# Earlier LayerNorm statistics, a lower load threshold, and a split first output group

## The chip, the cores and the metric

The kernel runs on all 8 cores of one Trainium2 chip. Each core works on its own 2,048 tokens of 4,096 features and no core talks to another, but the cores share the memory outside. The metric is device time in microseconds of the slowest core; smaller is better.

## The reference

```python
x = x + attn(layernorm(x))     # causal convolution over the last axis (4096) with an S4 kernel K, plus D * u
x = x + ffn(layernorm(x))
# ffn, with 64 experts of rank 16, top 16 of them by score:
scores = xf @ Wr.T
top_vals, top_idx = jax.lax.top_k(scores, TOPK)
gates = jax.nn.softmax(top_vals, axis=-1)
G = zeros(N, K).at[arange(N)[:, None], top_idx].set(gates)
h = einsum('nd,krd->nkr', xf, A)
out = einsum('nkr,kdr->nd', h * G[:, :, None], B) * 2.0
```

The convolution kernel K comes from 64 complex state values by a Cauchy sum. The kernel on the chip works out K by matrix powers instead (the setup below).

## The kernel before

The core's tokens are cut into four groups of 512 (`s` = 0 to 3), held transposed: features lie on the partitions as 32 blocks of 128, tokens along the row. Instructions are written out per engine by a small class `Plan`: each engine runs its own list strictly in the order of emission, with waits on counting semaphores put in by hand. `P.dma` with its default makes each transfer wait for the one before it on the same semaphore.

**Setup.** Small tables are loaded; then SP loads group 0 of the input, `U`, in four quarters of 8 blocks each (L381, semaphore `uld`, one after the other). Then some 200 small steps build the convolution matrices. Each is issued by `so(engine, fn)`, which waits for the step before it (semaphore `seq`), whatever its engine: a serial chain through VectorE and TensorE. The first 43 steps are VectorE's and one ScalarE's alone; step 44 is the first TensorE one, the matmul at L444. Steps 44 to 47 are matmuls, 48 and 49 the copies L448 and L449, 50 the matmul L452. Later ones that matter here: 60 is L467 and 61 L468, 62 is L469; 71 is L483, 72 is L484, 73 is L487; from 84 on, L502 and L504 are matrix products, each with a copy behind it (L503, L505), 12 times.

**Statistics of group 0.** `emit_prep1(0)` makes eight pieces, kept in the list `PRE0`. A piece covers four blocks. For each block ScalarE casts it to bf16 (L259), TensorE adds it up by a matmul (L264), GpSimd squares it (L272) and TensorE adds up the squares (L277). There are four cast buffers and two buffers for squares. `so` takes one piece from `PRE0` behind every 12th step, so pieces 1 to 3 are emitted ahead of step 44, and pieces 4 to 8 behind steps 48, 60, 72, 84 and 96. The result is needed only by `emit_chain1(0)`, after the last `so` step of the matrices.

**Stage 1** is the convolution for each group: matmuls (L688, L711), then VectorE scales and adds to `U` (L727, L732), and quarters are stored twice, as f32 `xsp_f` by ScalarE's queue (`spf`) and as bf16 `xsp_b` by GpSimd's (`spb`), 16 counts a quarter, 64 a group, 256 in all. The At matrix is loaded late in this stage.

**Stage 2** reads `xsp_b` back as `X`, into two buffers in turn: group 0 in two halves (L782, L788), groups 1 to 3 by L796 on SP's queue, in this order, each behind its own waits for `spf` and `spb`; from group 2 on it also waits until the matmuls of the buffer's last group are done (`t_h`). Scores, gating and the matmuls L978 give `htl_a` (rank blocks 0 to 3) and `htl_b` (4 to 7). L982 is the last product of each block of `t_h`.

**Stage 3** runs over eight half groups (`s2`), each 16 blocks `dd` of 128 features; a block is 8 matmuls of 512 columns (`kb` = 0 to 7, L1066), the first four with `Bt_lo` and the last four with `Bt_hi`, into one of two PSUM banks of `psA`; VectorE adds twice the result to `XF` (L1073). `Bt_hi` can be loaded only after the last stage 2 matmul, since it lies where At lay: GpSimd's queue does so in four transfers one after the other (L1031). `XF` is loaded from `xsp_f` by SP in quarters one after the other (L1045), two buffers; the whole half group is stored by L1078 when its 16 blocks are done, and the load of half group `s2` waits for the store of `s2 - 2`.

Of the kernel before, what the change touches and what calls it, by code (L numbers as in the profile page):

```python
# [9 lines left out]
ALU = mybir.AluOpType  # L10
# [3 lines left out]
DM = 4096  # L14
# [64 lines left out]
def build_nc():  # L79
# [32 lines left out]
    def alloc(name, shape, dtype, at=None):  # L112
        a = off[0] if at is None else at
        h = nc.alloc_sbuf_tensor_at(name, shape, dtype, offset=a)
        if at is None:
            sz = int(np.prod(shape[1:])) * (4 if dtype == F32 else 2)
            off[0] = a + ((sz + 127) // 128) * 128
        return h
# [50 lines left out]
    Bt_lo = alloc("Bt_lo", [128, 4 * DM], BF16, at=RW + 65536)  # L169
    Bt_hi = alloc("Bt_hi", [128, 4 * DM], BF16, at=RW)  # L170
# [7 lines left out]
    def htl_ap(kr, lo, hi):  # L178
        t = htl_a if kr < 4 else htl_b
        k = kr % 4  # L180
        return t.ap()[:, k * NTOK + lo:k * NTOK + hi]
# [17 lines left out]
    psA = nc.alloc_psum_tensor("psA", [128, 2048], F32)  # L199
# [5 lines left out]
    P = Plan(nc)  # L205
# [114 lines left out]
    PRE0 = []  # L320
    SO_CTR = [0]

    def so(eng, fn):
        P.wait(eng, "seq")
        P.wait(eng, "sqd")
        P.wait(eng, "sqg")
        P.op(eng, fn, inc="seq")
        SO_CTR[0] += 1
        if SO_CTR[0] % 12 == 0 and PRE0:
            PRE0.pop(0)()  # L330

    bload(lambda e: e.dma_start(out=identf.ap(), in_=identf_in.ap()))
# [52 lines left out]
    PRE0.extend(_steps0)  # L385

    so("vector", lambda e: e.memset(ONES64, 1.0))
    ONE1 = onesrf.ap()[0:1, 0:1]

    so("scalar", lambda e: e.activation(ss("step"), ss("ls"), AF.Exp))  # L390
    so("vector", lambda e: e.reciprocal(ss("istep"), ss("step")))
    so("vector", lambda e: e.tensor_scalar(ss("c0"), ss("istep"), 2.0, None, ALU.mult))
    so("vector", lambda e: e.tensor_scalar(ss("c4"), ss("istep"), 4.0, None, ALU.mult))
# [191 lines left out]
    for c in range(NCH):  # L585
# [4 lines left out]
        for tb in range(NSUB):  # L590
# [8 lines left out]
            for jb in range(tb + 1):  # L599
# [4 lines left out]
                    start=fst, stop=(jb == tb)), inc=("c1g" if jb == tb else None))  # L604
# [5 lines left out]
        for jb in range(NSUB):  # L610
# [3 lines left out]
                start=(jb == 0), stop=last0), inc=("c1t" if last0 else None))  # L614
# [32 lines left out]
    for s in range(NS1):  # L647
# [29 lines left out]
        for c in range(NCH):  # L677
# [7 lines left out]
            for jb in range(NSUB):  # L685
# [5 lines left out]
                    start=(jb == 0), stop=last0), inc=("t_sc" if last0 else None))  # L691
# [85 lines left out]
    for s in range(NS1):  # L777
        P.wait("sync", "spb", 64 * (s + 1))
        if s == 0:
            P.wait("sync", "spf", 208)  # L780
            P.wait("sync", "spb", 208)
            P.dma("sync", lambda e: e.dma_start(  # L782
                out=X2[0].ap()[:, 0:8192],
                in_=bass.AP(xsp_b, 0, [[NBLK * F1, 128], [1, 8192]])), "x2h")
            P.wait("sync", "spf", 224)
            P.wait("sync", "spb", 224)
            P.wait("sync", "x2h", 16)
            P.dma("sync", lambda e: e.dma_start(  # L788
                out=X2[0].ap()[:, 8192:16384],
                in_=bass.AP(xsp_b, 8192, [[NBLK * F1, 128], [1, 8192]])), "x2l")  # L790
            continue
        P.wait("sync", "spf", 256)
        P.wait("sync", "spb", 256)
        if s >= 2:
            P.wait("sync", "t_h", 8 * (s - 1))
        P.dma("sync", lambda e, s=s: e.dma_start(out=X2[s % 2].ap()[:, :], in_=xsp_b.ap()[s]), "x2l")  # L796
# [136 lines left out]
    for db in range(16, NBLK):  # L933
# [8 lines left out]
            inc=("t_a1" if db == NBLK - 1 else None))  # L942
# [13 lines left out]
    htl_after = []  # L956
# [7 lines left out]
    for s in range(NS1):  # L964
# [8 lines left out]
        for kr in range(8):  # L973
# [3 lines left out]
            for db in range(NBLK):  # L977
# [8 lines left out]
                start=False, stop=True), inc="t_h")  # L986
# [61 lines left out]
    for s2 in range(NS3):  # L1048
        s1, g = s2 // 2, s2 % 2
        xf = XF[s2 % 2]  # L1050
        for dd in range(16):
            d = 16 * g + dd
            pb = dd % 2
            if s2 == 0 and dd < 2:
                P.wait("tensor", "v_ht", htl_after[-1] - 1 + dd)
            if s2 * 16 + dd >= 2:
                P.wait("tensor", "v_y", P.count("v_y") - 1)
            for kb in range(8):
                bt = Bt_lo if kb < 4 else Bt_hi
                kbo = kb % 4  # L1060
                if s2 == 0 and dd == 0:
                    if kb == 0:
                        P.wait("tensor", "btl", 16 * 4)
                    else:
                        P.wait("tensor", "bhi", 16 * (kb - 4 + 1)) if kb >= 4 else None
                P.op("tensor", lambda e, d=d, kbo=kbo, kb=kb, pb=pb, s1=s1, bt=bt: e.matmul(  # L1066
                    psA.ap()[:, pb * 512:(pb + 1) * 512],
                    bt.ap()[:, kbo * DM + d * 128:kbo * DM + (d + 1) * 128],
                    htl_ap(kb, s1 * 512, (s1 + 1) * 512),
                    start=(kb == 0), stop=(kb == 7)), inc=("t_o" if kb == 7 else None))  # L1070
            P.wait("vector", "t_o")
            P.wait("vector", "xfl", 64 * s2 + 16 * (dd // 4 + 1))
            P.op("vector", lambda e, dd=dd, pb=pb, xf=xf: e.scalar_tensor_tensor(  # L1073
                xf.ap()[:, dd * 512:(dd + 1) * 512], psA.ap()[:, pb * 512:(pb + 1) * 512],
                2.0, xf.ap()[:, dd * 512:(dd + 1) * 512], ALU.mult, ALU.add), inc="v_y")
        dstap = bass.AP(y_out, s1 * 128 * (NBLK * F1) + g * 8192, [[NBLK * F1, 128], [1, 8192]])
        P.wait("scalar", "v_y")
        P.dma("scalar", lambda e, dstap=dstap, xf=xf: e.dma_start(out=dstap, in_=xf.ap()[:, :]), "yd")  # L1078
# [12 lines left out]
def _get_nc():  # L1091
    global _NC_CACHE
    if _NC_CACHE is None:
        _NC_CACHE = build_nc()
    return _NC_CACHE
# [52 lines left out]
```

How the kernel before makes its waits and increments, by code:

```python
    def wait(self, eng, name, val=None):  # L42
        self.sem(name)
        v = self.counts[name] if val is None else val
        if v <= 0:
            return
        h = self.sems[name]
        self.ops[eng].append(lambda e, h=h, v=v: e.wait_ge(h, v))
# [1 line left out]
    def op(self, eng, fn, inc=None, amt=1):  # L50
        if inc is not None:
            h = self.sem(inc)
            self.counts[inc] += amt
            self.ops[eng].append(lambda e, fn=fn, h=h, a=amt: fn(e).then_inc(h, a))
        else:
            self.ops[eng].append(lambda e, fn=fn: fn(e))
```

## Time and profile before

| | us |
|---|---|
| median of 2 runs | 1474.57 (1471.29 to 1477.85) |
| the profiled execution's own time | 1478.3 |
| its span on the slowest core (core 6) | 1476.6 |
| spans of the other cores | 1451.0 to 1474.9 |

| engine | busy us | share of the span |
|---|---|---|
| TensorE matmul | 995.4 | 67% |
| VectorE | 455.4 | 31% |
| ScalarE | 194.6 | 13% |
| GpSimd | 179.3 | 12% |

No engine is busy throughout, and the busy shares are means over stages with different limits. So the profile is read by stages, and in each stage by what is waited for last. A row of the chain gives the start, the length and the engine with its line; a row of the timeline gives the start, the length, the engine, the line, the instruction and how many of it were merged.

### The profile page before, as it was taken

The page shows a single profiled execution, that of the slowest core. Times are in us where ns is not written, and L with a number is a line of the kernel's source. Part 1 is how long each engine was busy: PE and PEld are TensorE (multiplying, and loading weights), DVE is VectorE, ACT ScalarE, POOL GpSimd, SP SyncE. Part 2 cuts the span into 40 slices and gives each one's busy share as a digit, 9 for nine tenths or more (in the row PEclk, how much of TensorE's full clock was granted, in tenths as well). Part 3 has the DMA queues.
Part 4 walks back from the last instruction along what each step waited for, and adds up shares of the span by engine and source line. Part 5 has one row for each costly group of instructions (what it writes and reads, how often), then busy time and mean ns, then how long its engine had stood idle before and what let it go on. Part 6 is the DMA issues. An engine that isn't in the chain of part 4 may idle for free.

```text
span 1476.6 us, 13267 instructions; the slowest of 8 cores (1451.0 to 1476.6 us)
## 1 busy us (share of the span) xinstructions
PE 995.4 (67%) x3837; PEld 396.3 (27%) x3837; DVE 455.4 (31%) x954; ACT 194.6 (13%) x402; POOL 179.3 (12%) x221
## 2 busy tenths in 40 slices
PE   1665337776775777334488678768869809998985
PEld 0233122221221222111123223322323304443432
DVE  2122116355364467104321222132130003433332
ACT  1300022433423322000100100010010000000000
POOL 6510000631513414000000000000000000000000
PEclk9655557888988989768589778777979959999998
DMA  6300008838638229986000110020015184777776
GB/s 116 137 0 0 7 16 289 273 108 261 224 131 239 87 86 213 191 186 207 0 1 0 72 43 1 0 114 1 0 24 92 35 218 159 270 257 249 263 243 242
DMA packets 25520, 186.59 MB, mean 126 GB/s; under 512 B 7592, under 2 KB 8361, under 8 KB 12522
## 3 DMA queue, kind: packets, MB, share of 16 engines
q1 hardware_dynamic: 9274, 84.52, 16.0%
q0 software_dynamic: 12720, 34.11, 13.4%
q10 hardware_dynamic: 3456, 67.11, 12.9%
q8 instruction: 34, 0.56, 0.2%
q14 instruction: 36, 0.29, 0.1%
HBM read 119.15 MB, written 83.89 MB: 137 GB/s over the span
## 4 chain that ended last, share of the span: by engine, by line
PE 37%; DMA 26%; DVE 11%; issue 9%; POOL 5%; another core or an unknown queue 5%; ACT 3%; DVEq 1%; ACTq 0%; POOLq 0%; SPq 0%
PE psA L978 16%; DMA XF<-xsp_f 13%; DMA xsp_b<-U 7%; POOL sqs L272 3%; DMA Bt_hi<-bt_in 3%; PE psA L1066 3%; PE ps L823 3%; DVE sqs L817 2%; PE psX L870 2%; PE ps L277 2%; DVE cvt L727 2%; PE ps L264 1%; PE psA L711 1%; DMA U<-u_in 1%
## 5 line engine op out<-in xcount | busy, mean ns | idle before, releaser
L978 PE MATMUL psA<-X,At_sb 128*128 128x512 bf16 x1024 | 255.1, 413 | 0.0
L1066 PE MATMUL psA<-htl_b,Bt_hi 128*128 128x512 bf16 x512 | 135.4, 387 | 41.2 <-DMA Bt_hi<-bt_in 41.2
L1073 DVE SCALAR_TENSOR_TENSOR XF<-psA,XF 128x512 f32<-128x512 f32 x128 | 88.2, 691 | 198.7 <-PE psA L1066 159.4
L1066 PE MATMUL psA<-htl_a,Bt_lo 128*128 128x512 bf16 x512 | 135.5, 388 | 16.5 <-DVE XF L1073 16.5
L978 PEld LDWEIGHTS psA<-X,At_sb 128*128 128x128 bf16 x1024 | 106.3, 105 | 140.8 <-issue 42.5
L272 POOL TENSOR_TENSOR sqs<-ubf 128x512 bf16<-128x512 bf16 x128 | 131.3, 1056 | 66.7 <-PE ps L277 51.4
L264 PE MATMUL ps<-ubf,sumw 128*128 128x512 bf16 x128 | 62.8, 491 | 72.4 <-ACT ubf L259 72.4
L259 ACT CAST ubf<-U 128x512 bf16<-128x512 f32 x128 | 73.6, 615 | 168.7 <-PE ps L264 65.0
L732 DVE TENSOR_TENSOR U<-U,cvt 128x512 f32<-128x512 f32 x128 | 89.9, 702 | 13.7 <-DVE cvt L727 0.5
L711 PE MATMUL psA<-ln1w,cm_T 128*128 128x512 bf16 x320 | 93.2, 390 | 0.0
L727 DVE TENSOR_TENSOR cvt<-psA,Rb 128x512 f32<-128x512 f32 x128 | 87.7, 685 | 7.1 <-PE psA L717 7.1
L277 PE MATMUL ps<-sqs,sumw 128*128 128x512 bf16 x128 | 60.2, 470 | 39.9 <-POOL sqs L272 39.5
L823 PE MATMUL ps<-sqs,sumw 128*128 128x512 bf16 x128 | 56.3, 488 | 39.7 <-DVE sqs L817 39.3
L668 ACT CAST ln1w<-U 128x512 bf16<-128x512 f32 x128 | 69.1, 614 | 93.4 <-PE psA L717 55.2
L1066 PEld LDWEIGHTS psA<-htl_b,Bt_hi 128*128 128x128 bf16 x512 | 50.9, 99 | 105.5 <-issue 47.4
L1066 PEld LDWEIGHTS psA<-htl_a,Bt_lo 128*128 128x128 bf16 x512 | 50.6, 100 | 80.3 <-issue 23.2
L817 DVE TENSOR_TENSOR sqs<-X 128x512 bf16<-128x512 bf16 x128 | 50.8, 423 | 44.5 <-PE ps L823 36.9
L696 DVE CAST state<-psS 128x512 bf16<-128x512 f32 x32 | 22.0, 688 | 136.7 <-PE psS L693 129.7
L1002 DVE TENSOR_TENSOR htl_a<-psA,grep 128x512 bf16<-128x512 f32 x16 | 11.1, 692 | 166.6 <-ACT grep L998 166.6
L1002 DVE TENSOR_TENSOR htl_b<-psA,grep 128x512 bf16<-128x512 f32 x16 | 11.1, 691 | 143.3 <-ACT grep L998 143.3
L773 POOL DMA_DIRECT2D Bt_lo<-bt_in x4 | 2.1, 546 | 425.3 <-PE psA L982 425.3
L717 PE MATMUL psA<-negmr,c1row 1*128 1x512 bf16 x128 | 50.6, 395 | 0.0
(228 smaller groups left out, 692.2 us busy)
## 6 DMA issues: line engine op xcount, KB each, us to landing
U<-u_in SPq DMA_DIRECT2D x16, 2048.0 KB, 9.1
xsp_f<-U ACTq DMA_DIRECT2D x16, 2048.0 KB, 13.4
XF<-xsp_f SPq DMA_DIRECT2D x32, 1024.0 KB, 5.8
y_out<-XF ACTq DMA_DIRECT2D x8, 4096.0 KB, 17.1
xsp_b<-U POOLq DMA_DIRECT2D x16, 1024.0 KB, 13.0
X<-xsp_b SPq DMA_DIRECT2D x3, 4096.0 KB, 14.1
At_sb<-at_in POOLq DMA_DIRECT2D x32, 256.0 KB, 55.1
X<-xsp_b SPq DMA_DIRECT2D x2, 2048.0 KB, 11.8
```

The lines of the kernel that those rows point to most:

```text
L259: P.op("scalar", lambda e, b=b, w=w: e.copy(UBF.ap()[:, w * 512:(w + 1) * 512], blk_ap(buf, b)), inc="s_ub")
L264: P.op("tensor", lambda e, b=b, w=w: e.matmul(ps1.ap()[:, :], sumw.ap()[:, :], UBF.ap()[:, w * 512:(w + 1) * 512], start=(b == 0), stop=(b ...
L272: P.op("gpsimd", lambda e, b=b, q=q, w=w: e.tensor_mul(sqs.ap()[:, q * 512:(q + 1) * 512], UBF.ap()[:, w * 512:(w + 1) * 512], UBF.ap()[:, ...
L277: P.op("tensor", lambda e, b=b, q=q: e.matmul(ps2.ap()[:, :], sumw.ap()[:, :], sqs.ap()[:, q * 512:(q + 1) * 512], start=(b == 0), stop=(b ...
L711: P.op("tensor", lambda e, tb=tb, w=wslot, d=tb - jb, fst=fst, bank=bank: e.matmul(psA.ap()[:, bank * 512:(bank + 1) * 512], cm_T.ap()[:, ...
L727: P.op("vector", lambda e, bank=bank, sl=sl, q2=q2: e.tensor_mul(cvt.ap()[:, q2 * 512:(q2 + 1) * 512], psA.ap()[:, bank * 512:(bank + 1) * ...
L732: P.op("vector", lambda e, b=b, buf=buf, q2=q2: e.tensor_add(blk_ap(buf, b), blk_ap(buf, b), cvt.ap()[:, q2 * 512:(q2 + 1) * 512]), inc="v ...
L817: P.op("vector", lambda e, b=b, q=q, xb=xb: e.tensor_mul(sqs.ap()[:, q * 512:(q + 1) * 512], blk_ap(xb, b), blk_ap(xb, b)), inc="v_sq")
L823: P.op("tensor", lambda e, b=b, q=q: e.matmul(ps2.ap()[:, :], sumw.ap()[:, :], sqs.ap()[:, q * 512:(q + 1) * 512], start=(b == 0), stop=(b ...
L978: P.op("tensor", lambda e, kr=kr, db=db, pb=pb, xb=xb: e.matmul(psA.ap()[:, pb * 512:(pb + 1) * 512], At_sb.ap()[:, db * 1024 + kr * 128:d ...
L1066: P.op("tensor", lambda e, d=d, kbo=kbo, kb=kb, pb=pb, s1=s1, bt=bt: e.matmul(psA.ap()[:, pb * 512:(pb + 1) * 512], bt.ap()[:, kbo * DM + ...
L1073: P.op("vector", lambda e, dd=dd, pb=pb, xf=xf: e.scalar_tensor_tensor(xf.ap()[:, dd * 512:(dd + 1) * 512], psA.ap()[:, pb * 512:(pb + 1) ...
```

## The change

There are three edits.

1. `so` takes a piece of the statistics behind every 5th step instead of every 12th, up to step 45. All eight pieces are then emitted behind steps 5, 10, ... 40, so before step 44 in every engine's list.
2. The load of `X` for even groups from 2 on waits for 224 counts of `spf` and `spb` instead of 256.
3. In the first half group of stage 3, the first four blocks `dd` run their four `Bt_lo` products ahead, into four PSUM banks, and then their four `Bt_hi` products; blocks 4 to 15 and all other half groups stay as they were.

```diff
-        if SO_CTR[0] % 12 == 0 and PRE0:
+        if SO_CTR[0] % 5 == 0 and SO_CTR[0] <= 45 and PRE0:
             PRE0.pop(0)()
...
-        P.wait("sync", "spf", 256)
-        P.wait("sync", "spb", 256)
+        need = 224 if s % 2 == 0 else 256
+        P.wait("sync", "spf", need)
+        P.wait("sync", "spb", need)
...
-        for dd in range(16):
+        if s2 == 0:
+            for dd in range(4):
+                if dd < 2:
+                    P.wait("tensor", "v_ht", htl_after[-1] - 1 + dd)
+                if dd == 0:
+                    P.wait("tensor", "btl", 16 * 4)
+                for kb in range(4):
+                    P.op("tensor", lambda e, dd=dd, kb=kb: e.matmul(
+                        psA.ap()[:, dd * 512:(dd + 1) * 512],
+                        Bt_lo.ap()[:, kb * DM + dd * 128:kb * DM + (dd + 1) * 128],
+                        htl_ap(kb, 0, 512), start=(kb == 0), stop=False))
+            for dd in range(4):
+                for kb in range(4, 8):
+                    if dd == 0:
+                        P.wait("tensor", "bhi", 16 * (kb - 3))
+                    P.op("tensor", lambda e, dd=dd, kb=kb: e.matmul(
+                        psA.ap()[:, dd * 512:(dd + 1) * 512],
+                        Bt_hi.ap()[:, (kb - 4) * DM + dd * 128:(kb - 4) * DM + (dd + 1) * 128],
+                        htl_ap(kb, 0, 512), start=False, stop=(kb == 7)),
+                        inc=("t_o" if kb == 7 else None))
+                P.wait("vector", "t_o")
+                P.wait("vector", "xfl", 16)
+                P.op("vector", lambda e, dd=dd, xf=xf: e.scalar_tensor_tensor(
+                    xf.ap()[:, dd * 512:(dd + 1) * 512], psA.ap()[:, dd * 512:(dd + 1) * 512],
+                    2.0, xf.ap()[:, dd * 512:(dd + 1) * 512], ALU.mult, ALU.add), inc="v_y")
+        for dd in range(4 if s2 == 0 else 0, 16):
             d = 16 * g + dd
             pb = dd % 2
-            if s2 == 0 and dd < 2:
-                P.wait("tensor", "v_ht", htl_after[-1] - 1 + dd)
```

## Rows read from the trace of the kernel before

**Rows 1.** Busy time by stage: stretch, length, engines' busy us (instructions), clock, DMA share, GB/s.
```profile
45.60:218.30 172.70, 86.88 (x368) 50.59 (x367) 36.38 (x127) 17.55 (x61) 20.01 (x21) 0.52 0.05 19
...
1218.90:1476.60 257.70, 227.03 (x1017) 100.85 (x1017) 88.17 (x128) 0.00 (x0) 0.00 (x0) 0.94 0.69 241
```

**Rows 2.** Timeline of SP, VectorE, ScalarE in the setup: the loads and first waits.
```profile
21.19 27.73 SPq L381 DMA_DIRECT2D U<-u_in  x4
...
47.89 0.22 DVE L448 COPY smat<-psA 64x64 f32<-64x64 f32 x1 [21.25 <-PE psA L447]
...
48.72 1.21 ACT L259 CAST ubf<-U 128x512 bf16<-128x512 f32 x2 [2.92 <-DMA U<-u_in]
```

**Rows 3.** DMA issues from 48 to 60 us: the last quarter, us to landing.
```profile
U<-u_in SPq DMA_DIRECT2D x1, 2048.0 KB, 8.1
```

**Rows 4.** Timeline of GpSimd in the setup: the squares, two of their seven stretches.
```profile
32.02 8.08 POOL L272 TENSOR_TENSOR sqs<-ubf 128x512 bf16<-128x512 bf16 x8 [13.39 <-ACT ubf L259]
...
48.89 4.03 POOL L272 TENSOR_TENSOR sqs<-ubf 128x512 bf16<-128x512 bf16 x4 [2.02 <-PE ps L277]
```

**Rows 5.** Chain of work in the setup: TensorE's steps of the chain behind each piece.
```profile
45.61 0.41 PE psA L444 x2
...
51.66 0.31 PE psX L452 x2
...
59.48 0.41 PE psX L469 x2
...
66.96 0.33 PE psX L487 x2
...
77.16 0.78 PE psA L502 x2
...
88.91 0.47 PE psA L504 x2
```

**Rows 6.** Timeline of VectorE in the setup: the copies that the chain could go on from.
```profile
48.21 0.22 DVE L449 COPY smat<-psA 64x64 f32<-64x64 f32 x1
...
55.71 0.22 DVE L468 TENSOR_TENSOR smat<-psX,identf 64x64 f32<-64x64 f32 x1 [0.70 <-PE psX L467]
...
60.31 0.84 DVE L396 TENSOR_TENSOR smat<-smat 64x64 f32<-64x64 f32 x2
...
63.30 0.29 DVE L484 COPY Xt<-psA 128x128 f32<-128x128 f32 x1 [0.70 <-PE psA L483]
...
67.64 0.67 DVE L489 TENSOR_SCALAR Sch<-Xt,dcol 128x128 f32<-128x128 f32 x1
...
72.53 0.29 DVE L503 COPY Sch<-psA 128x128 f32<-128x128 f32 x1 [1.02 <-PE psA L502]
76.73 0.29 DVE L505 COPY Tch<-psA 128x128 f32<-128x128 f32 x1 [3.90 <-PE psA L504]
```

**Rows 7.** Timeline of SP's queue in stage 2: loads of X, groups 1 and 2.
```profile
680.95 0.32 SPq L796 DMA_DIRECT2D X<-xsp_b  x1
840.28 0.32 SPq L796 DMA_DIRECT2D X<-xsp_b  x1
```

**Rows 8.** Timeline at the start of stage 3: TensorE's products.
```profile
1218.86 0.59 PE L1066 MATMUL psA<-htl_b,Bt_hi 128*128 128x512 bf16 x1 [10.65 <-DMA Bt_hi<-bt_in]
1219.24 1.91 PE L1066 MATMUL psA<-htl_a,Bt_lo 128*128 128x512 bf16 x4
...
1225.07 1.03 PE L1066 MATMUL psA<-htl_a,Bt_lo 128*128 128x512 bf16 x4
```

**Rows 9.** Chain of work from 1240 us: the first store and what follows.
```profile
1248.63 11.80 DMA y_out<-XF
1260.55 5.72 DMA XF<-xsp_f
```

**Rows 10.** Short stretches of clock and DMA: setup, then the start of stage 3.
```profile
100.00:200.00 100.00, 42.39 (x116) 27.54 (x116) 23.86 (x79) 0.00 (x0) 0.00 (x0) 0.50 0.01 3
...
1237.00:1240.00 3.00, 3.00 (x16) 1.35 (x15) 1.38 (x2) 0.00 (x0) 0.00 (x0) 1.00 0.00 0
```

More of the change, by code:

```diff
@@ L1060, in build_nc @@
                 kbo = kb % 4
[L1061 to L1065, printed above, removed]
                 P.op("tensor", lambda e, d=d, kbo=kbo, kb=kb, pb=pb, s1=s1, bt=bt: e.matmul(
```

## The prediction

> **What bounds the kernel now.** I read the table of cores first, to see that all eight run alike, then the busy time cut into stages, then the chain of work that ended last, and last the timelines of single engines around the three places that the change touches.
>
> The busy time by stage [rows 1] shows a setup of 172.7 us, from the first TensorE step of the matrix chain to the end of the matrices, in which TensorE is busy half the time at a granted clock of 0.52 and the DMA engines stand at 0.05. That is a serial chain of small steps: its length is the number of steps times the latency of each, and whatever is queued on TensorE between two steps adds to it. The last stretch, 257.7 us, has TensorE and DMA at work together: a half group's load, products and store follow each other, and the chain there runs through loads and stores.
>
> **Edit 1, the statistics pieces.** It removes no instruction. It moves five pieces of four blocks each from behind steps 48, 60, 72, 84 and 96 to ahead of step 44.
>
> What the five cost today is read from the chain. The step that could have gone on had its copy done early, and TensorE's next chain step starts only after the piece. From a copy's end to the next matmul the chain needs 0.14 us. Piece 4: L449 ends at 48.21 + 0.22 = 48.43, so L452 could start at 48.57; it starts at 51.66: 3.09 us [rows 5, 6]. Piece 5: L468 ends at 55.93, L469 could start at 56.07 and starts at 59.48: 3.41. Piece 6: L484 ends at 63.59, L487 could start at 63.73 and starts at 66.96: 3.23. Piece 7: VectorE is idle 3.90 us before the copy L505 where it is idle 1.02 before the copy L503 one step earlier [rows 6]: 2.88. Piece 8 shows the same pair, 3.90 and 1.02, behind step 96: 2.88. Sum 15.49 us given back.
>
> Two small corrections. GpSimd's squares run beside two VectorE instructions of the chain: L489 takes 0.67 us where its like takes 0.29, and the pair L396 takes 0.84 for what is 0.22 each elsewhere [rows 6]. That goes away with the squares: 0.8 us more saved. Against it, right behind piece 8 three matmul lines (one stands in [rows 5]) take 0.47 us instead of the 0.78 behind piece 7 [rows 5], since the clock is up for a moment: 0.9 us lost. Saved in all: 15.49 + 0.8 - 0.9 = 15.4 us.
>
> What is queued behind the moved pieces is L444, step 44, on TensorE. VectorE had long finished step 43 when it waited 21.25 us for the matmuls L444 to L447 [rows 2], which stood behind pieces 1 to 3. After the change they stand behind all eight. When is the eighth done? The quarters of U land one after the other: SP issues four from 21.19, the last one at 21.19 + 27.73 - 0.35, about 48.6; the third quarter is what ScalarE waits for until 48.72 [rows 2], and the last lands 8.1 us after its issue [rows 3], at 56.7. GpSimd is the pace of a piece, 8.08 us for 8 blocks and 4.03 for 4, so 1.01 us a block [rows 4]. A cast takes 1.21 / 2 = 0.61 [rows 2]; with 0.15 for the two hand-overs (an estimate, from the 0.14 above) the third quarter's squares start at 49.48. The last quarter lands before GpSimd is through with the third (57.55), so 16 blocks run without a gap: 49.48 + 16 x 1.0075 = 65.6. The last product of squares starts 0.14 later and takes 0.59 as a like one at the half clock does [rows 8], so L444 starts at about 66.3 instead of 45.61 [rows 5]. That is 20.7 us lost.
>
> Edit 1 is therefore 20.7 - 15.4 = +5.3 us. The reason in one sentence: five pieces that cost 3.1 us each in the chain, because GpSimd and ScalarE had worked ahead under VectorE's steps, now cost the full 1.01 us per block in front of it. Bounds: if the chain had been ready to lose nothing it would be -15.4; with no clock correction and no relief on VectorE it is +5.2; if the last quarter landed late, each microsecond beyond 57.5 adds one.
>
> A rule of the skill bears on the clock here. The Trainium skill, "TensorE: Matmul & The Clock Gate", section on the clock gate, says that the default state is throttled and activity releases the throttle. By it a run of pieces without a break would end at the upper level, and the first chain steps behind it would take 0.47 instead of 0.78. The trace shows both: 0.47 behind piece 8 and 0.78 behind piece 7 [rows 5]. By the rule the sum for this edit is about +4.
>
> **Edit 2, the threshold.** Only group 2 gets 224. SP runs its list in order: the load of group 1 waits for all 256 and is issued at 680.95, and the load of group 2 comes behind it, at 840.28, released by the products of stage 2 [rows 7]. When SP comes to the wait for 224, 256 is long reached. No instruction is added or taken. Cost 0, and nothing to bound: the counters never fall.
>
> **Edit 3, the split output group.** Behind the last stage 2 product TensorE runs four Bt_lo products and then waits for each of four Bt_hi transfers; the last lands for the product at 1218.86, after 10.65 us of waiting for it alone [rows 8]. After the change 16 Bt_lo products run in that gap, 12 more. The work that hides them is the transfer: even at the half clock, 1.91 us per four, they take 7.6 us, less than such a wait. Behind 1218.86 there are then 12 products fewer. Which products are saved? The clock in the trace is at half level for the first 13 products after the wait, 0.43 us apart, and then at full level: four every 0.86 us, 0.2155 us apart [rows 8]. After the change the 13 products left for blocks 0 to 3 (one, then twelve) take the same half-clock stretch, and the full-clock products that follow are 12 fewer: 12 x 0.2155 = 2.6 us. If half-clock products were saved instead it would be 12 x 0.43 = 5.2. I take 2.6. The Trainium skill, same page and section, says that the warm-up is a matter of time, not of a number of matmuls; by it too full-clock products fall away. VectorE needs 0.69 us a block and gets one every 1.7 us in the half-clock stretch, so it doesn't fall behind; banks 2 and 3 of psA are free by then.
>
> Does it reach the end? The store of half group 0 is issued at 1248.63, when its last block is done, and the load of half group 2 follows that store at 1260.55 [rows 9]. Before the store the DMA engines are idle: share 0.00 at 1237 to 1240 [rows 10]. So an earlier store starts earlier, and the chain behind it, in which loads wait for stores, moves as a whole: -2.6 us. The bound above is 0, if the DMA engines' work is what counts.
>
> **The sum.** +5.3 + 0 - 2.6 = +2.7 us. The profiled execution took 1478.3 us, of which 1476.6 is the span; it would take 1481.0. It lies 3.7 above the median of the runs, 1474.57; against that median the forecast is 1477.3.
>
> **The rivals.**
> - *The clock rises before the chain.* The setup's matrix products between 100 and 200 us run at 0.50 with TensorE busy 42% of the time [rows 10]. Were the clock up behind the run of pieces, the first three or four chain steps would save 0.31 each, about 1.2 us: 1476.1. Were it up for all 37 half-clock pair products of L502, L504 and the four rounds behind them, 37 x 0.31 = 11.5 us: 1466. Against the latter: piece 8's own burst left nothing of it in those 100 us. Chance 0.12. The page's rule on the clock gate speaks for the small end.
> - *Edit 3 does not reach the end.* Stage 3 moves 241 GB/s at a DMA share of 0.69 [rows 1]; if transfers of all cores set its length, the 2.6 us are waited off at the next load: 1479.9. Chance 0.13.
> - *Edit 1 pays.* If TensorE could run L444 in time, the pieces would be free and 15.4 + 2.6 us would be won: 1456.6. The wait of 21.25 us speaks against it: there L444 was already held behind three pieces. Chance 0.04.
> - *Slower, by the input load.* L444 now waits for the last quarter of U. If the eight cores' loads take longer, each microsecond beyond 57.5 adds one. It decides against "within 2%" only at +29.5 us in all, a last quarter landing at about 84, three times the 8.1 us it took. Against it: the DMA engines have little else to do in the setup, share 0.05 behind 45.6 us [rows 1]. Chance 0.03 for any sizeable part of it.
>
> **How the numbers follow.** The forecast has 0.68. The single edits are a few microseconds and the two runs of before alone are 6.6 apart, so the range takes the cases with 1466 and 1480 and the spread of the runs on both sides: 1465 to 1487. Faster or slower by more than 2% (29.5 us, about what a measurement can tell from no change) needs one of the last two rivals with much more than its price: 0.02 and 0.02. Within 2%: 0.96.
>
> **What would show it.** Edit 1 right: L444 starts near 66 instead of 45.6, with no L264 or L277 behind it, and the setup ends 5 us later than at 218.3. Wrong: L444 earlier than 62, or chain steps at 0.47 for long. Edit 2: the load of X for group 2 still follows the stage 2 product. Edit 3 right: 16 products before the first wait for Bt_hi, and from the last Bt_hi landing to the first store 27.2 us instead of 29.8; wrong, if the first load behind the store does not move with it. The prediction fails if the stages between, which the change does not touch, move by more than the setup's shift.

## The result

The changed kernel takes 1479.46 us (median), the kernel before 1475.51 in the same comparison. The ratio is 1.0024, 95% interval 1.0012 to 1.0035: 1.8 to 5.2 us slower, 3.5 in the middle. By the 2% bound that is no change. The forecast was +2.7 us, within 2%. Ratios here and below are taken over the fast executions alone (in two of the changed kernel's 43, four or all of the cores ran at a lower clock and the time was 1515 us), so they are not always the quotients of the medians. The profiled execution took 1478.5 us; its longest core is core 3, with 1477.0. Core 6, whose rows were read before, is shown here so that like stands beside like; its span is 1474.4.

GpSimd's timeline on core 6, in the setup (start, length, instruction, count, idle before it):

```profile
30.78 8.06 POOL L272 TENSOR_TENSOR sqs<-ubf 128x512 bf16<-128x512 bf16 x8 [12.19 <-ACT ubf L259]
40.17 8.02 POOL L272 TENSOR_TENSOR sqs<-ubf 128x512 bf16<-128x512 bf16 x8 [1.32 <-ACT ubf L259]
48.91 8.01 POOL L272 TENSOR_TENSOR sqs<-ubf 128x512 bf16<-128x512 bf16 x8 [0.73 <-PE ps L277]
57.25 8.02 POOL L272 TENSOR_TENSOR sqs<-ubf 128x512 bf16<-128x512 bf16 x8 [0.33 <-ACT ubf L259]
```

Four stretches of eight blocks, one for each quarter of U, where before there were seven [rows 4]. Each takes 8.0 us, so within a quarter GpSimd sets the pace. The gaps between them, 2.4 us in all, are mostly the load of U: ScalarE, which casts ahead of GpSimd, waits for the second and the last quarter to land.

```profile
39.34 2.69 ACT L259 CAST ubf<-U 128x512 bf16<-128x512 f32 x5 [3.62 <-DMA U<-u_in]
...
56.43 2.70 ACT L259 CAST ubf<-U 128x512 bf16<-128x512 f32 x5 [2.79 <-DMA U<-u_in]
```

TensorE's timeline on core 6 goes on from there:

```profile
65.42 0.38 PE L277 MATMUL ps<-sqs,sumw 128*128 128x512 bf16 x1 [0.41 <-POOL sqs L272]
65.72 0.32 PE L444 MATMUL psA<-vrow 1*64 1x64 f32 x2
66.19 0.29 PE L445 MATMUL psA<-vrow 1*64 1x64 f32 x2
66.64 0.44 PE L446 MATMUL psA<-vrow 1*64 1x64 f32 x2
```

L444 follows the last product of squares. The chain of work on core 6 behind it:

```profile
65.79 0.27 PE psA L444 x2
...
68.10 0.23 DVE smat L449
68.46 0.35 PE psX L452 x2
...
72.56 0.23 DVE smat L468
72.92 0.46 PE psX L469 x2
...
76.48 0.30 DVE Xt L484
76.92 0.57 PE psX L487 x2
...
82.98 0.78 PE psA L504 x2
83.86 0.30 DVE Tch L505
```

Each of these matmuls now starts 0.13 to 0.14 us behind its copy. From L444 to L487 it is 11.1 us; before it was 21.4 [rows 5]. SP's queue on core 6 in stage 2, and TensorE at the start of stage 3 there:

```profile
680.72 159.47 SPq L797 DMA_DIRECT2D X<-xsp_b  x2
```

```profile
1176.15 2.75 PE L1059 MATMUL psA<-htl_a,Bt_lo 128*128 128x512 bf16 x12 [0.70 <-DVE htl_b L1003]
1186.59 0.58 PE L1067 MATMUL psA<-htl_b,Bt_hi 128*128 128x512 bf16 x1 [7.69 <-DMA Bt_hi<-bt_in]
...
1219.01 5.23 PE L1067 MATMUL psA<-htl_b,Bt_hi 128*128 128x512 bf16 x13 [9.68 <-DMA Bt_hi<-bt_in]
1224.08 1.03 PE L1085 MATMUL psA<-htl_a,Bt_lo 128*128 128x512 bf16 x4
```

The load of group 2 goes out 159 us behind that of group 1, as before [rows 7]. Twelve more Bt_lo products lie in the wait; the 13 products from the last Bt_hi on take 5.1 us to the next start, 1224.08, nearly all at the half clock, and from there it is four every 0.86 us [rows 8].

The cores differ from each other and from execution to execution by more than the change moves. So I took four marks from the timelines of all eight cores and averaged each over the cores: the start of L444; the second load of U, SP's first issue behind the setup; the first product that uses the last part of Bt_hi; the first store of the output.

| mean over 8 cores, us | before | after |
|---|---|---|
| L444 starts | 43.7 | 64.6 |
| from there to the second load of U | 172.2 | 157.7 |
| second load of U | 215.9 | 222.2 |
| from there to the last Bt_hi product | 996.7 | 994.8 |
| last Bt_hi product to the first store | 29.4 | 27.0 |
| first store to the end | 227.0 | 227.4 |

Lost in front of L444: 20.9. Given back in the chain: 14.5. Saved in stage 3: 2.4. Together +4.0 us. The stretch from the second load of U to the last Bt_hi product, stages 1 and 2, is not touched by the change. It is 1.9 us shorter in this execution, and lies between 993.2 and 996.1 us in those of the kernels below: that is scatter, less than the setup's shift. With it the mean end of the cores moves by +2.4 us, 1469.0 to 1471.4.

### The profile page after: what moved, and what is told of

The parts are those of the page before. It is cut to its first block, busy times and chain, and to the rows that moved or that the text cites. A ratio compares the mean times of both kernels' runs of the same rounds, so it can differ in the third digit from the quotient of the medians.

```text
span 1477.0 us, 13265 instructions; the slowest of 8 cores (1461.2 to 1477.0 us)
## 1 busy us (share of the span) xinstructions
PE 994.8 (67%) x3837; PEld 396.3 (27%) x3837; DVE 454.8 (31%) x954; ACT 194.2 (13%) x402; POOL 178.7 (12%) x221
## 4 chain that ended last, share of the span: by engine, by line
PE 41%; DMA 21%; DVE 11%; issue 10%; POOL 6%; another core or an unknown queue 5%; ACT 4%; DVEq 1%; ACTq 0%; POOLq 0%; SPq 0%
PE psA L979 15%; DMA XF<-xsp_f 8%; PE psA L1085 6%; DMA xsp_b<-U 6%; POOL sqs L272 4%; DMA Bt_hi<-bt_in 3%; PE ps L824 3%; DVE sqs L818 2%; PE psX L871 2%; PE psA L711 2%; DVE cvt L727 2%; PE psS L688 1%; PE ps L277 1%; DMA y_out<-XF 1%
## 5 line engine op out<-in xcount | busy, mean ns | idle before, releaser
L1085 PE MATMUL psA<-htl_a,Bt_lo 128*128 128x512 bf16 x496 | 129.4, 384 | 15.7 <-DVE XF L1092 15.7
L272 POOL TENSOR_TENSOR sqs<-ubf 128x512 bf16<-128x512 bf16 x128 | 130.9, 1054 | 43.9 <-PE ps L277 30.2
L1085 PE MATMUL psA<-htl_b,Bt_hi 128*128 128x512 bf16 x496 | 128.8, 382 | 0.0
L264 PE MATMUL ps<-ubf,sumw 128*128 128x512 bf16 x128 | 58.5, 457 | 65.9 <-ACT ubf L259 65.9
L277 PE MATMUL ps<-sqs,sumw 128*128 128x512 bf16 x128 | 55.9, 437 | 50.7 <-POOL sqs L272 50.6
L824 PE MATMUL ps<-sqs,sumw 128*128 128x512 bf16 x128 | 55.9, 484 | 39.9 <-DVE sqs L818 39.6
L1085 PEld LDWEIGHTS psA<-htl_a,Bt_lo 128*128 128x128 bf16 x496 | 48.7, 99 | 76.8 <-issue 20.5
L1003 DVE TENSOR_TENSOR htl_a<-psA,grep 128x512 bf16<-128x512 f32 x16 | 11.1, 692 | 164.9 <-ACT grep L999 164.9
```

The costliest lines, as they stand in the source:

```text
L272: P.op("gpsimd", lambda e, b=b, q=q, w=w: e.tensor_mul(sqs.ap()[:, q * 512:(q + 1) * 512], UBF.ap()[:, w * 512:(w + 1) * 512], UBF.ap()[:, ...
L277: P.op("tensor", lambda e, b=b, q=q: e.matmul(ps2.ap()[:, :], sumw.ap()[:, :], sqs.ap()[:, q * 512:(q + 1) * 512], start=(b == 0), stop=(b ...
L824: P.op("tensor", lambda e, b=b, q=q: e.matmul(ps2.ap()[:, :], sumw.ap()[:, :], sqs.ap()[:, q * 512:(q + 1) * 512], start=(b == 0), stop=(b ...
```

## The experiments

Each expectation was written before its kernel ran. "Ratio" is to the kernel before on the same chip, with its 95% interval. The marks come from one profiled execution of each kernel. e6, e7, e10 and e11 have no ratio, and marks alone are read of them. Comments in the diffs are mine.

| mean over 8 cores, us | L444 | L444 to second load of U | second load of U | last Bt_hi to first store | first store to end |
|---|---|---|---|---|---|
| before | 43.7 | 172.2 | 215.9 | 29.4 | 227.0 |
| e1 | 64.3 | 157.6 | 221.9 | 29.6 | 227.9 |
| e2 | 44.0 | 172.0 | 216.0 | 29.6 | 229.0 |
| e3 | 44.2 | 172.0 | 216.1 | 26.9 | 228.3 |
| e4 | 43.9 | 157.0 | 200.8 | 29.2 | 228.6 |
| e5 | 44.5 | 172.2 | 216.7 | 23.4 | 231.4 |
| e6 | 44.9 | 173.2 | 218.0 | 25.8 | 231.8 |
| e7 | 27.1 | 189.5 | 216.6 | 29.4 | 228.1 |
| e8 | 27.1 | 159.6 | 186.7 | 29.6 | 227.0 |
| e9 | 27.1 | 159.5 | 186.6 | 23.8 | 229.3 |
| e10 | 52.6 | 165.3 | 217.9 | 29.6 | 228.7 |
| e11 | 44.2 | 171.9 | 216.0 | 24.9 | 225.8 |

**The three edits one by one.** e1 is the kernel before with

```diff
-        if SO_CTR[0] % 12 == 0 and PRE0:
+        if SO_CTR[0] % 5 == 0 and SO_CTR[0] <= 45 and PRE0:
```

> Edit 1 alone: all eight statistics pieces ahead of step 44. Theory (each moved piece costs 1.01 us a block in front of L444 and gives back 3.1 us in the chain): +5.3 us, ratio 1.0036; L444 starts near 66 on core 6 and the first c1row transfer comes 5 us later than at 216.4. Rival A (the pieces off the chain are a gain): 15 us less, ratio 0.990. Rival B (the clock is up behind the run of pieces for longer): +4 or less, with many products at 0.47 us.

Measured: ratio 1.0039 (1.0018 to 1.0060), about +5.8 us of 1475. The marks give +20.6 in front of L444, -14.6 in the chain: +6.0. Edit 1 alone is the loss. Rival A is out by its sign; rival B is out too: by the marks the sum is above +5.3, not below, and the 24 matrix steps L502 and L504 follow each other every 1.31 us on all cores, as at the half clock before (the times alone, +2.7 to +8.8 us, would not exclude its +4).

e2 has only the lower threshold:

```diff
-        P.wait("sync", "spf", 256)
-        P.wait("sync", "spb", 256)
+        need = 224 if s % 2 == 0 else 256
```

> Edit 2 alone: the load of X for group 2 waits for 224 counts instead of 256. Theory: nothing, since SP's list has the load of group 1 with its wait for 256 ahead; ratio 1.000, and the load of group 2 is still issued behind the stage 2 product. Rival: the load starts earlier and stage 2 gains.

Measured: 0.9995 (0.9973 to 1.0017), and none of the first four marks in the table moves by more than 0.3 us. The runs allow -4.0 to +2.5 us; that it is nothing rests on the order in SP's list, where the wait for 256 comes first, and on the issue times: in e2 on core 6 the load of group 2 goes out 157 us behind that of group 1, before 159 us [rows 7].

e3 has only the split of the first four blocks:

```diff
+        if s2 == 0:
+            for dd in range(4):     # kb 0 to 3 of each block
...
+            for dd in range(4):     # kb 4 to 7 of each block
```

> Edit 3 alone: four blocks with Bt_lo ahead. Theory: 12 full-clock products less behind the last Bt_hi, -2.6 us, ratio 0.9982; from the last Bt_hi product to the first store about 27.2 us. Rival A: the stage is set by transfers, 0. Rival B: half-clock products are saved, -5.2 us.

Measured: 0.9988 (0.9968 to 1.0008), -1.8 us with an interval from -4.7 to +1.2; the mark falls by 2.5 us, 29.4 to 26.9. The mark decides for the full-clock count and against rival B. The time alone can't tell -2.6 from 0.

**What a piece costs, by where it lies.** e7 puts all eight pieces behind the last matrix step:

```diff
-        if SO_CTR[0] % 12 == 0 and PRE0:
+        if False:
             PRE0.pop(0)()
```

> The kernel before with all eight pieces behind the last matrix step, so that none lies in the chain or in front of L444. Theory: L444 starts at about 26.8 (VectorE's step 43 and 0.14) instead of 43.7 on the mean of cores; the chain itself is as short as with edit 1; then the 32 blocks run at 1.01 us each in front of the statistics, 28 of them in the open. From L444 to the second load of U: 172.2 - 14.5 + 30 = 188 us, second load of U at 215, as before within 3 us. Rival (the chain is short after edit 1 only because the clock or VectorE profits from the early pieces): 10 us later.

Measured: L444 at 27.1, 189.5 us from there, second load of U at 216.6. GpSimd's timeline on core 1, the longest, shows where the 30 us are:

```profile
30.85 2.04 POOL L272 TENSOR_TENSOR sqs<-ubf 128x512 bf16<-128x512 bf16 x2 [12.28 <-ACT ubf L259]
163.68 4.08 POOL L272 TENSOR_TENSOR sqs<-ubf 128x512 bf16<-128x512 bf16 x4 [130.78 <-PE ps L277]
167.98 25.95 POOL L272 TENSOR_TENSOR sqs<-ubf 128x512 bf16<-128x512 bf16 x26 [0.23 <-issue]
```

Two squares are made early, the other 30 run at 1.0 us each from 163.68 to 193.9 with almost nothing else on the way. It was to be 28 in the open, with four worked ahead; it is 30. So pieces in front of the chain and pieces behind it cost the same, GpSimd's full pace, and the chain itself is no faster for having them early. The rival is out: it asked for 10 us more, and the second load of U came 0.7 us later than before.

e10 moves five pieces ahead instead of eight:

```diff
-        if SO_CTR[0] % 12 == 0 and PRE0:
+        if (SO_CTR[0] in (7, 14, 21, 28, 35) or SO_CTR[0] in (72, 84, 96)) and PRE0:
```

> Five pieces ahead of step 44 (behind steps 7, 14, 21, 28, 35), the last three behind steps 72, 84 and 96 as before. Theory (each moved piece takes 4 x 1.01 = 4.0 us in front of L444, the GpSimd having worked two blocks ahead, and gives 3.1 back): L444 at about 52 on the mean of cores against 43.7, the chain 6.5 us shorter than 172.2, the second load of U at about +2 against 215.9. Rival (the loss of edit 1 comes from waiting for the last quarter of U alone): no loss or a gain with five ahead, since these need three quarters only.

Measured: L444 at 52.6, +8.9; the chain 165.3, -6.9; second load of U at 217.9, +2.0. This kernel needs only three quarters of U ahead of L444, and still loses 2 us with two pieces moved, where edit 1 loses 6 with five. The exchange is about 1.0 to 1.2 us lost per piece moved. So waiting for the last quarter of U is not what makes the loss. (Its one execution took 1485.7 us on the slowest core, which tells nothing by itself: on the mean of cores it ended at 1470.7 us, against 1469.0 before.)

e4 leaves the first three pieces in place and puts the other five into the setup's small transfers, during which TensorE waits:

```diff
-        if SO_CTR[0] % 12 == 0 and PRE0:
+        if SO_CTR[0] in (12, 24, 36) and PRE0:
...
     sd(lambda e: e.dma_start(out=kp_dram.ap(), in_=kp_sb.ap()))
+    PRE0.pop(0)()
...
         sd(lambda e, s=src: e.dma_start(out=Xt[2].ap()[:, :], in_=s))
+        PRE0.pop(0)()
```

> The kernel before, but pieces 4 to 8 are emitted behind the five small transfers of the setup (kp_dram and four reads of it), where TensorE stands idle some 3.5 us each, instead of behind steps 48 to 96. Theory (pieces cost because they lie between two chain steps): the 15.4 us of pieces 4 to 8 go, each leaves about 0.4 us in its new place: -13 us, ratio 0.991, L444 still at 45.6. Rival (the setup's end is set otherwise, or a piece takes longer there because GpSimd and ScalarE do not keep up): 0 to -5 us.

Measured: 0.9884 (0.9861 to 0.9908), -17.1 us (-20.5 to -13.6); the second load of U comes 15.1 us earlier. The chain takes 157.0 us with five pieces in it; with none in it (e1) it takes 157.6. So in the waits they cost nothing in sum, where I had expected 2 us. TensorE's timeline on core 3 shows a reason:

```profile
140.22 0.61 PE L264 MATMUL ps<-ubf,sumw 128*128 128x512 bf16 x1
...
143.58 0.38 PE L277 MATMUL ps<-sqs,sumw 128*128 128x512 bf16 x1
143.90 0.46 PE L553 MATMUL psA<-Xt,jrev 128*128 128x128 f32 x2
...
155.54 0.38 PE L277 MATMUL ps<-sqs,sumw 128*128 128x512 bf16 x1 [0.41 <-POOL sqs L272]
155.77 0.46 PE L553 MATMUL psA<-Xt,jrev 128*128 128x128 f32 x2
156.95 0.30 PE L562 MATMUL psA<-identf,Vch 128*128 128x128 f32 x1 [0.72 <-DVE cm_T L559]
```

From 143.6 on, a product of a piece lasts 0.38 instead of 0.61 us, and the chain's own products behind the pieces (L553, L562) run shorter too: the clock came up within the pieces. On the mean of cores it is 0.7 us less than in e1 from the first to the fourth small read, and 0.5 less behind; ahead of the reads the chain is 0.5 longer. So the faster clock paid for what the pieces still cost.

e8 goes one step further. No piece lies ahead of L444; the first 12 blocks' 24 products go one by one behind the 24 matmul steps L502 and L504, the other 20 blocks into the waits of e4:

```diff
-        if SO_CTR[0] % 12 == 0 and PRE0:
+        if FINE[0] and eng == "tensor" and PRE0:   # FINE: only in the loop of L502 to L505
             PRE0.pop(0)()                          # one product, with its cast or square
...
+    for _ in range(8):                             # behind each of the five transfers
+        PRE0.pop(0)()
```

> No piece ahead of L444. The first 12 blocks' 24 products go one each behind the 24 matmul steps L502 and L504, where TensorE stands idle 0.53 us while VectorE copies; the other 20 blocks go into the five transfer waits as in e4. Theory (what a piece costs is what exceeds TensorE's idle time where it lies): L444 at 26.8 instead of 43.7, -17, and the chain as in e4, -15: -32 us, ratio 0.978. Rival (a product of 0.43 us between two steps costs what it lasts): 24 x 0.43 = 10 us less gain, ratio 0.985.

Measured: 0.9793 (0.9753 to 0.9833), -30.6 us (-36.5 to -24.7); whether it passes 2% is open. L444 at 27.1, the chain 159.6. TensorE and VectorE on core 4:

```profile
53.16 0.77 PE L545 MATMUL psA<-Tch,Sch 128*128 128x128 f32 x2
...
53.72 0.63 PE L315 MATMUL ps<-sqs,sumw 128*128 128x512 bf16 x1
54.03 0.29 DVE L546 COPY Tch<-psA 128x128 f32<-128x128 f32 x1 [1.02 <-PE psA L545]
54.47 0.76 PE L543 MATMUL psA<-Sch,Tch 128*128 128x128 f32 x2
```

A step follows the one before it in 1.31 us (53.16 to 54.47), which is exactly the step of the kernel before without a piece in it, and the product L315 lies between them, while VectorE copies. The rival's ten us for the 24 products would make the chain 167 us; it is 2.6 us longer than e4's 157.0. From the first to the last of the 24 copies it is 30.14 us on the mean of cores, and it is 30.14 in e1 and 30.13 in e7, which have no product there: the 24 products cost nothing. Of the 2.6 us, 1.2 lie ahead of the first of these steps, and e7 has them too: without pieces ahead the first steps run at the half clock, and a square that GpSimd makes early stretches the VectorE step L460 to 0.84 us (e7, core 1), where after has 0.25.

**How much of the split reaches the end.** e5 takes edit 3 from four blocks to eight, with psS, ps1, ps2 and psX as the other banks:

```diff
-            for dd in range(4):
+            for dd in range(8):
...
-                        psA.ap()[:, dd * 512:(dd + 1) * 512],
+                        banks[dd],
```

> Edit 3 taken further: eight blocks, not four, run their four Bt_lo products ahead, into the four banks of psA and psS, ps1, ps2, psX, which stage 3 does not use. Theory (the saving is the number of products taken from behind the last Bt_hi, at the full clock): 28 x 0.2155 = 6.0 us from the last Bt_hi product to the first store against before, so 23.4 us on the mean of cores where before has 29.4; the end moves by as much, ratio 0.996. Rival A (transfers set the stage): the first store is 6 us earlier and the stretch from it to the end is that much longer, ratio 1.000. Rival B (VectorE is late, a block every 0.86 us against its 0.69): half of it.

Measured: 0.9949 (0.9922 to 0.9977), -7.5 us with an interval from -11.5 to -3.4. The mark falls by 6.0, as 28 full-clock products make it, so VectorE is not late. From the first store to the end its profiled execution has 231.4 us; those of the kernels with an unchanged stage 3 lie from 227.0 (before, e8) to 229.0 (e2). That points to some 2 to 4 us given back to the transfers, the times point to nothing given back. The later stores tell how far the gain is certain. On the mean of cores the second and the third store follow the first by 27.7 and 55.3 us in every kernel, in e5 too, so the 6 us are still whole at the third. The fifth follows by 118.5 to 119.9 us in the kernels with an unchanged stage 3, and by 122.2 in e5, 121.1 in e3 and 121.3 in e9, but by 119.4 in after and 115.9 in e11, which are split as well. So what becomes of the gain behind the third store is not settled: rival A in full is out by the times, and in part it may stand.

**Why the products behind the last Bt_hi are at the half clock.** e6 and e11 are e3 with extra products into an unused bank in the waits; e11 only has more of them:

```diff
+                        for _ in range(NDUM[kb - 4]):   # e6 (26, 36, 36, 36), e11 (30, 46, 46, 46)
+                            P.op("tensor", lambda e: e.matmul(
+                                ps1.ap()[:, :], sumw.ap()[:, :], Bt_lo.ap()[:, 0:512],
+                                start=True, stop=True, skip_group_check=True))
                         P.wait("tensor", "bhi", 16 * (kb - 3))
```

> Edit 3 with 134 extra products into the unused bank ps1 in the four waits for Bt_hi (26, 36, 36, 36), so that TensorE is busy most of the time. Theory (the 13 products behind the last Bt_hi run at the half clock because the engine stood idle): they take 0.2155 us instead of 0.43, and the stretch from the last Bt_hi product to the first store falls from 26.9 (edit 3 alone) to 24.1 us. Rival (VectorE or something else sets them): 26.9 as before.

> e6 with more extra products in the waits for Bt_hi (30, 46, 46, 46), so that TensorE stands idle under 1 us ahead of the last Bt_hi instead of 2.4 to 2.9. In e6 the 13 products took 3.0 to 3.3 us on three cores and 4.4 to 4.8 on five. Theory (the clock falls in the idle time left): 3.0 to 3.3 on all eight cores, and 24.9 us to the first store. Rival: a mix as in e6.

Groups of products by shape, busy us, mean ns and idle time before them; the first line is e6 on core 4, the second e6 on core 1, both the 13 products behind the last Bt_hi:

```profile
L1073 PE MATMUL psA<-htl_b,Bt_hi 128*128 128x512 bf16 x13 | 3.0, 379 | 2.4 <-DMA Bt_hi<-bt_in 2.4
L1073 PE MATMUL psA<-htl_b,Bt_hi 128*128 128x512 bf16 x13 | 4.7, 535 | 2.7 <-DMA Bt_hi<-bt_in 2.7
```

In e6 three cores (2, 4, 6) have all of them at 378 or 379 ns, and their first store comes 24.94 us behind the last Bt_hi product; the other five have 505 to 536 ns on the mean. In e11 it is 378 or 379 ns on all eight cores. So it is TensorE's standing idle in the waits that puts these products at the half clock, and filling the waits takes it away. The last idle time alone does not tell a core's outcome, though: core 2 of e6 stood idle 3.2 us and kept the clock, core 1 stood 2.7 us and lost it, and on core 6 of e11 the last two waits left 1.9 and 1.7 us and did no harm; there my expectation of under 1 us was not met. It is worth 2.0 us at the first store (26.9 to 24.9), where I had expected 2.8 of e6, and takes 168 extra products. The reason for the difference is in e3: its granted clock comes back 3.2 to 5.9 us behind the last Bt_hi product, by core, so on most cores fewer than 13 products are at the half clock.

**The best version.** e9 is e8 and e5 together.

> e8 and e5 together: products between the setup's matrix steps and in its transfer waits, and eight blocks split at the start of stage 3. Theory: the shifts add, -32 at the start of stage 1 (e8 measured -29.2 on the mean of cores) and -6 at the first store: -35 us, ratio 0.976. Rival (stage 3's transfers take the second part back): as e8 alone, 0.979.

Measured: 1442.41 us against 1477.85, ratio 0.9755 (0.9722 to 0.9788), -36 us. It beats the kernel before by more than 2%, and with after at 1.0024 of before it beats that too. Its marks are those of e8 and e5 to 0.4 us.

## Why the prediction was right

**Edit 1, the delay of L444.** Forecast 20.7 us on core 6 (45.61 to 66.3); there it was 65.79, 20.2, and 20.9 on the mean of cores. GpSimd's pace held (8.0 us for 8 blocks, four times), and L444 came straight behind. That it fits core 6 so well is in part luck: the third quarter's squares began 0.6 us earlier than forecast, the last product took 0.38 us for 0.59, and against these the last quarter of U came 0.33 us too late to leave no gap. The bound in the prediction, each microsecond beyond 57.5, forgot the cast and the hand-overs: by its own numbers it is 57.55 less 0.76, 56.8. On four cores (0, 3, 5, 7) the load kept ahead, there is no gap at all and L444 starts at 62.2 to 63.6; on the other four the gaps add to 1.3 to 2.8 us and it starts at 65.6 to 66.7. So GpSimd sets the delay on half of the cores, and the load of U adds to it on the others. e7 and e10 show the same pace from the other side.

**Edit 1, what the chain gets back.** Forecast 15.4, measured 14.5 on the mean of cores (14.6 in e1). I took it apart by the starts of VectorE's copies, up to the write of kp_dram. On the mean of cores the five pieces gave back 14.8 us where the prices add to 15.49. Most of the difference is piece 4: core 6, which the rows are from, had its full 3.1 us, and the cores lie between 2.3 and 3.1. The relief on VectorE is 0.5 net, for 0.8: on core 6 L489 fell to 0.29 us as forecast, but the pair L396 only to 0.54, since that is what two of them take from start to end, and part of the rest went to the clock, as the next paragraph shows. The clock behind piece 8 cost 1.1 for 0.9. With 0.1 at L444 to L447 the sum is 14.3; the small reads of kp_dram were 0.2 us shorter. On core 6 alone it is 14.9 up to kp_dram, and then the reads took 3.0 to 3.1 us three times, where they had taken 2.7; on the mean of cores they did not get longer.

A term is missing in the forecast: the clock was up behind piece 6 as well, on six of the eight cores. TensorE's timeline on core 6, the first two lines before, the last two after:

```profile
66.89 0.38 PE L487 MATMUL psX<-vrow,onesrf 1*128 1x1 f32 x2
69.64 0.24 PE L495 MATMUL psX<-wtv,smat 64*64 64x1 f32 x2 [2.37 <-DVE Tch L396]
...
76.92 0.55 PE L487 MATMUL psX<-vrow,onesrf 1*128 1x1 f32 x2 [0.54 <-DVE Xt L484]
79.46 0.34 PE L495 MATMUL psX<-wtv,smat 64*64 64x1 f32 x2 [1.99 <-DVE Tch L396]
```

With piece 6 gone these run at the half clock, which takes 0.4 us from what core 6 got back (it is contained in the figures above). The row of L487 at 0.33 us [rows 5] was there to be read.

The clock was up for only two matmuls behind the run of pieces on core 6, L444 and L445, so the rival of the clock gave back 0.3 us there and not 1.2 to 11.5; on the mean of cores the steps L444 to L447 are 0.1 us shorter than before, since on most cores they ran at the upper level before as well. The Trainium skill, "TensorE: Matmul & The Clock Gate", section on the clock gate, has activity release the throttle; the trace agrees at the end of the run (0.38 for L277 at 65.42), but on core 6 nothing of it was left one microsecond later (0.44 for L446 at 66.64), so the rule changed no sum.

**Edit 1 in sum.** Forecast +5.3, by marks +6.3 (after) and +6.0 (e1), by times +5.8 (2.7 to 8.8). The term that was sized too large is the second: 15.4 us for 14.5.

**Edit 2.** Forecast 0, and the issue order stands (e2).

**Edit 3.** Forecast -2.6 from 12 full-clock products; the mark says -2.4 and -2.5 (e3), and -6.0 for 28 (e5). That 13 products are at the half clock is core 6's case: before, the granted clock came back 2.9 to 6.0 us behind the last Bt_hi product, by core. Seven to 14 products start ahead of its return there, so all that are saved are full-clock products, but for one on two cores. That the saving reaches the end was assumed from idle DMA engines before the first store. The first load behind the store followed it by 12.6 us before and by 13.1 after on the mean of cores, so it moved with the store less half a microsecond. The comparison of after with e1, 1.0024 to 1.0039, differs by 2.2 us in the right direction, within the intervals of both.

**The sum.** Forecast +2.7; measured +3.5 (1.8 to 5.2). In time, 1477.3 was forecast and 1479.46 measured; 0.9 of these 2.2 us is that before itself came out at 1475.51 and not 1474.57.

**The rivals.** "Edit 1 pays" fell with e1; what it described exists, but where TensorE is idle (e4, e8), not in front of L444. The late input load happened in the small, by the 1.3 to 2.8 us of gaps on half of the cores. A landing at 84, as in that rival, would be 35 us behind the issue and so over four times the 8.1 us, not three times. "Edit 3 does not reach the end" is not fully out, as said at e5.

## What to carry to other kernels

Work that is moved out of a serial chain is not free until it has a place where its engine would stand idle: in front of the chain and behind it the pieces cost GpSimd's pace of 1 us a block, between two steps what exceeds the idle time, 3.1 us for eight products, and one product per step nothing (30.14 us for the same steps with 24 products and without). Look in the timeline for the idle time of the engine that issues in order, and cut the work to that size: the same pieces, only placed otherwise, made +6 (e1), -17 (e4) and -31 us (e8). And before lowering a threshold, read which wait stands ahead of it in the same queue.

## What the runs showed of the hardware

The granted clock in the profile can read full while the products run at the half rate. Stretches of e7 on core 1 and of e8 on core 4 (length, busy times, then the clock):

```profile
60.00:120.00 60.00, 31.70 (x86) 20.04 (x86) 16.05 (x55) 0.00 (x0) 0.00 (x0) 1.00 0.00 0
```

```profile
45.60:76.00 30.40, 27.11 (x69) 11.82 (x68) 7.24 (x25) 7.13 (x12) 12.00 (x12) 1.00 0.25 96
```

The clock column says 1.00 in both, and the pairs L502 and L504 take 0.78 us in the one (e7's chain of work) and L543 and L545 0.77 in the other, as they do at 0.50 before [rows 5, 10]; at the upper level they take 0.47. In both traces the first change of the clock on record is a rise, at 167.6 us in e7 and at 127.1 us in e8, and the column reads 1.00 for all that lies ahead of it. So the mean clocks of 0.84 to 0.85 that e7, e8 and e9 list are no gain; the durations of a known product tell the level. And in e8's stretch TensorE is busy 27.1 us of 30.4, and its products stay at the half rate to the end of it; I had expected neither. What in the engine's work brings the clock up, no run here separates.
